# Two of 216 sender columns read from a projection kept on the chip, in place of two gathers

## The chip, the cores and the metric

One Trainium2 chip, one of its cores. The metric is the device time of one execution in microseconds (us); lower is better. The kernel is written by hand in an assembler-like language: every engine (TensorE = PE, VectorE = DVE, ScalarE = ACT, GpSimd = POOL, SyncE = SP) has its own program, and the programs meet at semaphores alone.

## The reference

A graph of 12500 nodes with 64 features each and 412500 edges (sender `src`, receiver `dst`, sorted by receiver). Two layers; the second is the one that matters here:

```
x = x + h + segment_sum(gated_mlp(edge_attr), dst)         # layer 0, h = relu(layernorm(x))
h = relu(layernorm(x))                                     # layer 1
s_proj = h @ Ws + bs ; r_proj = h @ Wr + br                # per node, 64 features (4 heads of 16)
se, re = s_proj[src], r_proj[dst]                          # per edge
logits = sum_d mish(se + re) * aw + ab                     # per edge and head
alpha = softmax of the logits over the edges of a receiver
x = x + segment_sum(alpha * se, dst)
```

`s_proj[src]` has random rows: each edge needs 64 floats (256 bytes) from some row of the table.

## The kernel before, in words

The kernel has four stages, one function each. `edge_mlp` (from the start to about 1095 us) does the gated MLP. `update_nodes` (to about 1346 us) ends layer 0, projects the nodes in 14 steps (NS) of 7 x 128 nodes, writes the sender half to the table `s_proj` in DRAM (SP, L747) and scatters the receiver half into `sums` (POOL, L762). `attention` (to about 5297 us) goes over the edges, and `finish` gathers the results.

In `attention` partition p holds 3224 consecutive edges. They are worked on in 135 chunks (CA); a chunk is 24 columns (TA), a column being one edge of each of the 128 partitions. Three buffers (B) rotate: `se` takes the 24 sender rows of each partition, `rs` the receiver rows. The loop over `s` runs 14 times (SB), and its body is written out for 3 times 3 chunks, so one iteration, called a round here, is 9 chunks or 216 columns. Three chunks go before the loop (FIRST), six after it (LAST_TWO).

Who does what for chunk c:

- POOL (`gather`, L1039 to L1048): waits until DVE has used the buffer (`se_used`) and until ACT has copied the indices, then issues one indirect DMA for each column of the chunk, each of which fetches 128 rows of 256 bytes.
- In six of the nine chunks of a round (PATTERN), the last column isn't gathered by POOL. SP and ACT load 16 row addresses at a time from `picks` into registers and issue one DMA of one row per edge into `fetched` (`fetch`, L994 and L1142: SP 5 of the 8 groups of 16, ACT the other 3), and ACT copies it into its column of `se` (L1192). `picks` holds these indices, loaded by SP in `update_nodes` (L737 to L744).
- DVE (`body`, L1249): `mish` of chunk c (L1260), then `receivers` of chunk c+1 (L1224 to L1235: it waits for `keepf_ready`, which PE's `spread_keep` gives, and scans), then `add_senders` of chunk c+1 (L1247: it waits for the gathers of that chunk, `gathered`, and for `placed`), then the softmax part of chunk c (L1266 to L1293), in which L1282 is the last reader of the sender rows and frees the buffer. The program order is fixed: nothing of a chunk can pass what stands before it.
- ACT: tanh, ln, tanh for mish (L1129, L1135, L1137), exp (L1174), copies for POOL's indices and for the stores.
- PE: `spread_keep(c+1)` (L1079) and `logits(c)` (L1088), both after `mish` of c.

In `update_nodes` a projection step is: DVE normalises 896 nodes (L822 to L838), PE transposes them (L779), ACT copies that into `hT` (L808), PE multiplies by the two weights (L784), DVE adds the bias into `sr` (L848). `sr` has four buffers, each of which has to be both stored by SP and scattered by POOL before step k+4 writes it (L843 to L845). SP's program loads `src`, then the columns of `picks`, then stores the 14 parts of the table.

Of the kernel before, what the change touches and what calls it, by code (L numbers as in the profile page):

```python
# [21 lines left out]
P = 128  # L22
N = 12500
F = 64
# [42 lines left out]
ACT_FIRST = [(0, j, g) for j in range(LEAD) for g in range(SHARE, P // GANG)]  # L67
BIG = 1e30
# [24 lines left out]
class Body:  # L93
# [22 lines left out]

    def landed(self, b):

        if isinstance(self.s, int) and self.s < 0:
            return 16 * TA  # L120
        every = sum(at[1] == b for at in PATTERN)
        here = sum(at[1] == b and at[0] <= self.u for at in PATTERN)
        if isinstance(self.s, int) and self.chunk(b) >= CA - 2:
            here += TA - TL - ((self.u, b) in PATTERN)
        return self.s * (16 * (TA * ROUND - every)) + 16 * (TA * (self.u + 2) - here)
# [5 lines left out]
def column_of(m):  # L131

    s, j = divmod(m, NPICK)
    u, b = PATTERN[j]
    return (Body(s, u).chunk(b) + 1) * TA - 1

# [536 lines left out]
def update_nodes(nc, R, A, D, gathered0):  # L673


    with ExitStack() as ctx:
# [45 lines left out]
        sr_ready = sem("sr_ready")  # L722
        tabled = [sem(f"tabled{b}") for b in range(SR)]
# [3 lines left out]
        s_tab = D["s_proj"].rearrange("(j p) f -> p j f", p=P)  # L727

        @block.sync
        def _(sp):  # L730
            sp.wait_ge(padded, 1)
            src = A["src"][0:(P - 1) * RUN].rearrange("(p k) -> p k", k=RUN)
            sp.dma_start(R["src"][0:112, :], src[0:112, :]).then_inc(src_in, 16)
            sp.dma_start(R["src"][112:P - 1, :], src[112:P - 1, :]).then_inc(src_in, 16)
            sp.dma_start(R["src"][P - 1:P, 0:LAST * T], A["src"][(P - 1) * RUN:E].rearrange("(a k) -> a k", a=1)).then_inc(src_in, 16)
            sp.wait_ge(padded, 2)
            for m in range(PICKS):  # L737
                column = A["src"][column_of(m)::RUN]
                even = column.shape[0] // GANG
                sp.dma_start(R["picks"][0:even, m, :], column[0:even * GANG].rearrange("(g q) -> g q", q=GANG), allow_slow_non_contiguous=True)\  # L740
                    .then_inc(picks_in, 16)
                if column.shape[0] < P:
                    sp.dma_start(R["picks"][even:even + 1, m, 0:GANG - 1], column[even * GANG:P - 1].rearrange("(g q) -> g q", g=1),
                                 allow_slow_non_contiguous=True).then_inc(picks_in, 16)  # L744
# [4 lines left out]
            sp.wait_ge(picks_in, 16 * (PICKS + sum(column_of(m) + (P - 1) * RUN >= E for m in range(PICKS))))  # L749
            for b in range(SR):  # L750
                sp.wait_ge(tabled[b], 16 * len(range(b, NS, SR)))
# [20 lines left out]
        @block.tensor  # L772
        def _(pe):
            nc.tensor.matmul(half_ps[:, 0:F], R["half_state"][:, :], R["ident"][0:F, 0:F], start=True, stop=True).then_inc(half_in_ps, 1)
            for k in range(NS):
                pe.wait_ge(h_ready, k + 1)
                wait(pe, hT_ready, k * len(JQ))
                for j in range(JB):
                    last = nc.tensor.transpose(hT_ps[:, j // 4, (j % 4) * P:(j % 4 + 1) * P], hh[k % 2][:, j, :], R["ident"][:, :])  # L779
                last.then_inc(hT_in_ps, 1)  # L780
                pe.wait_ge(hT_ready, (k + 1) * len(JQ))
                wait(pe, sr_ready, k)
                for j in range(JB):
                    last = nc.tensor.matmul(pr_ps[:, j // 4, (j % 4) * P:(j % 4 + 1) * P], hT[:, j, :], R["wsr"][:, :], start=True, stop=True)  # L784
                last.then_inc(pr_in_ps, 1)

        @block.scalar
        def _(act):
# [8 lines left out]
            act.wait_ge(eps_ready, 2)  # L797
            for k in range(NS // 2):
# [5 lines left out]
            for k in range(NS):  # L804
                act.wait_ge(hT_in_ps, k + 1)
                wait(act, pr_in_ps, k)
# [3 lines left out]
                if k + 1 < NS:  # L810
                    root(k + 1)

        @block.vector
        def _(dve):
# [39 lines left out]
            nc.vector.memset(R["picks"][:, :, :], 0).then_inc(padded, 1)  # L854
            pairs = [slice(2 * JB * k, 2 * JB * (k + 1)) for k in range(NS // 2)]
# [29 lines left out]
def attention(nc, R, A, D, gathered0, state_rows, states_in):  # L885

    with ExitStack() as ctx:
# [35 lines left out]
        fetched = [sb(f"fetched{j}", [P, F]) for j in range(NPICK)]  # L923
        rows = state_rows
        den = [sb(f"den{b}", [P, H, TA]) for b in range(B)]
        held_ps, ex_bank, work_ps, lg_bank = ps("held_ps", [P, 3 * 512]), ps("ex_bank", [P, 512]), ps("work_ps", [P, 3 * 512]), ps("lg_bank", [P, 512])
# [14 lines left out]
        placed = sem("placed")  # L941
        heads_in = sem("heads_in")
# [28 lines left out]
        state_out = sem("state_out")  # L971
# [66 lines left out]
        def _(pool):  # L1038
            def gather(at, b):  # L1039
# [6 lines left out]
                for k in range(EARLY if first and b == 0 else 0, TA - 1 if at.picks(b) else width(c)):  # L1046
# [18 lines left out]
        def _(pe):  # L1065
# [25 lines left out]
            def body(at, last=False):  # L1091
                for b in range(B):
# [6 lines left out]
                    logits(c)  # L1099

            pe.wait_ge(prepared, 1)
# [10 lines left out]
        def _(act):  # L1112
# [42 lines left out]
            def body(at, last=False):  # L1155
# [7 lines left out]
                for b in range(B):  # L1163
# [24 lines left out]
                    if not (last and b + 2 >= B) and ahead.picks(b2):  # L1188
# [3 lines left out]
                        nc.scalar.activation(se[b2][:, TA - 1, :], fetched[j][:, :], ACT.Copy).then_inc(placed, 1)  # L1192
                    states = rows[b][:, 0:w, 0:H * HE].rearrange("p t (h e) -> p t h e", e=HE)
# [4 lines left out]
            act.sem_inc(placed, NPICK)  # L1198
            act.wait_ge(prepared, 1)
# [12 lines left out]
        def _(dve):  # L1212
            flat = lambda x: x.rearrange("p f t -> p (f t)")
            STEP = 15

# [21 lines left out]
            def add_senders(at, b, more=True):  # L1237
# [11 lines left out]
            def body(at, last=False):  # L1249
                for b in range(B):  # L1250
# [73 lines left out]
            nc.vector.tensor_copy(R["state"][:, 0:H * HE], nlast[:, :, :].rearrange("p h e -> p (h e)")).then_inc(state_out, 1)  # L1324
            nc.vector.tensor_copy(R["state"][:, H * HE:ROW], narrow(mx[(CA - 1) % B], TL)[:, :, TL - 1]).then_inc(state_out, 1)
            dve.wait_ge(state_out, 2)


def finish(nc, R, A, D, out, states_in, ABW=F + H):

    with ExitStack() as ctx:
# [27 lines left out]
        pe_do = [sem(f"pe_do{k}") for k in range(4)]  # L1359
        pe_did = [sem(f"pe_did{k}") for k in range(4)]  # L1360
        act_do = [sem(f"act_do{k}") for k in range(2)]
        act_did = [sem(f"act_did{k}") for k in range(2)]
# [35 lines left out]
        def _(pe):  # L1398
            ident = R["ident"]
            pe.wait_ge(pe_do[0], 1)  # L1400
            nc.tensor.transpose(a_ps[0:H, 0:P], R["state"][:, F + H:ROW], ident[:, :])  # L1401
            nc.tensor.transpose(b_ps[0:H, 0:P], drop[:, :], ident[:, :]).then_inc(pe_did[0], 1)
            pe.wait_ge(pe_do[1], 1)
            nc.tensor.transpose(a_ps[:, 0:H], mx_t[:, 0:P], ident[0:H, 0:H])  # L1404
            nc.tensor.transpose(b_ps[:, 0:H], mx_t[:, 1:P + 1], ident[0:H, 0:H]).then_inc(pe_did[1], 1)
            pe.wait_ge(pe_do[2], 1)
            nc.tensor.transpose(a_ps[0:ABW, 0:P], add[:, :], ident[:, :])  # L1407
            nc.tensor.transpose(b_ps[0:ABW, 0:P], mul[:, :], ident[:, :]).then_inc(pe_did[2], 1)
            pe.wait_ge(pe_do[3], 1)
            nc.tensor.transpose(a_ps[:, 0:ABW], cin_t[:, 0:P], ident[0:ABW, 0:ABW]).then_inc(pe_did[3], 1)  # L1410

        @block.scalar
        def _(act):
            for k in range(2):
                act.wait_ge(act_do[k], 1)
                nc.scalar.activation(e[:, :, :], e[:, :, :], ACT.Exp).then_inc(act_did[k], 1)  # L1416

        @block.vector
        def _(dve):
# [10 lines left out]
            nc.vector.tensor_scalar(drop[:, :], R["whole"][:, :].to_broadcast([P, H]), -1.0, BIG, ALU.add, ALU.mult).then_inc(pe_do[0], 1)  # L1430
            dve.wait_ge(pe_did[0], 1)
            do(nc.vector.tensor_copy(drop_t[:, :], b_ps[0:H, 0:P]))  # L1432
            nc.vector.tensor_tensor_scan(mx_t[:, 1:P + 1], drop_t[:, :], a_ps[0:H, 0:P], -BIG, ALU.add, ALU.max).then_inc(pe_do[1], 1)  # L1433
            dve.wait_ge(pe_did[1], 1)
# [5 lines left out]
            nc.vector.tensor_tensor(e[:, 1, :], R["state"][:, F + H:ROW], mio[:, 1, :], ALU.subtract).then_inc(act_do[0], 1)  # L1440
            dve.wait_ge(act_did[0], 1)
# [3 lines left out]
            nc.vector.tensor_tensor(by_head(add[:, :]), by_head(R["state"][:, 0:ABW]), heads_wide(e[:, 1, :]), ALU.mult).then_inc(pe_do[2], 1)  # L1445
            dve.wait_ge(pe_did[2], 1)
            do(nc.vector.tensor_copy(mul_t[:, :], b_ps[0:ABW, 0:P]))  # L1447
            nc.vector.tensor_tensor_scan(cin_t[:, 1:P + 1], mul_t[:, :], a_ps[0:ABW, 0:P], 0.0, ALU.mult, ALU.add).then_inc(pe_do[3], 1)  # L1448
            dve.wait_ge(pe_did[3], 1)
# [5 lines left out]
            nc.vector.tensor_tensor(e[:, 1, :], mio[:, 0, :], mt[:, :], ALU.subtract).then_inc(act_do[1], 1)  # L1455
            dve.wait_ge(act_did[1], 1)
# [20 lines left out]
def gnn_program(nc, A, out):  # L1477
# [8 lines left out]
    with ExitStack() as ctx:  # L1486
# [10 lines left out]
        edge_mlp(nc, R, A, D)  # L1497
        gathered0 = ctx.enter_context(nc.semaphore("agathered0"))
# [30 lines left out]
```

## Time and profile before

| | us |
|---|---|
| three executions | 5441.60, 5443.22 (median), 5446.89 |
| the profiled execution, its own time | 5442.07 |
| its span from first to last instruction | 5439.8 |
| busy: DVE / POOL / ACT / PE | 3909.6 / 3573.8 / 2555.2 / 2022.2 |

The span is 2.3 us less than the time of the same execution, which is 1.15 us below the median. In a row of the trace a group of instructions has its busy time, the mean of one in ns, and the idle time of its engine just before it with what ended that idle time ("issue" means that nothing that the profile shows ended it: the engine was between two of its own instructions). The timeline gives start, duration, engine, line, operation, output<-input. A DMA row on SPq or ACTq is the time of issuing it, not of the transfer.

### The profile page before, as it was taken

To read this page: it belongs to the slowest core of one execution; us is meant where nothing else is said; L and a number is where in the kernel's file an instruction comes from. 1 tells how busy PE (TensorE), PEld (TensorE's weight loads), DVE (VectorE), ACT (ScalarE), POOL (GpSimd) and SP (SyncE) were. 2 spreads that over 40 slices of the span, in tenths; PEclk is the share of its full clock that TensorE was granted. 3 is DMA by queue.
4 is the path that set the end of the run, shared out by engine and by line. 5 is a ranking of instruction groups with operands and counts; after the bars stand their busy time and mean duration, and the time that the engine had idled before them with its cause. 6 is when DMAs were issued, how large, how long until landed. Compare 5 with 4: busy or idle time off the path is not lost. (4 is left out here: it accounts for less than half of the span.)

```text
span 5439.8 us, 79208 instructions
## 1 busy us (share of the span) xinstructions
PE 2022.2 (37%) x13638; PEld 1308.1 (24%) x13638; DVE 3909.6 (72%) x4216; ACT 2555.2 (47%) x3324; POOL 3573.8 (66%) x3669
## 2 busy tenths in 40 slices
PE   8999999923112222222212212212212212222220
PEld 3444444412112212212212212212212212212220
DVE  6999988853577777777776777777777777777772
ACT  7999999911243343343343443443443443343440
POOL 2444430077777777777777777777777777777756
PEclk9999999955555655656555556556556556555555
DMA  8888888721333333333333333333333333333322
GB/s 215 266 261 265 263 261 267 246 49 44 81 89 89 82 84 89 85 81 89 82 84 89 79 87 89 81 85 89 79 87 90 77 89 89 79 88 89 78 67 51
DMA packets 331213, 630.53 MB, mean 116 GB/s; under 512 B 131947, under 2 KB 135556, under 8 KB 330590
## 3 DMA queue, kind: packets, MB, share of 16 engines
q1 hardware_dynamic: 204558, 501.63, 28.6%
q0 software_dynamic: 117456, 124.66, 12.9%
q10 hardware_dynamic: 8832, 1.15, 0.2%
q14 instruction: 356, 2.92, 0.2%
q8 instruction: 11, 0.18, 0.0%
HBM read 391.98 MB, written 235.04 MB: 115 GB/s over the span
## 5 line engine op out<-in xcount | busy, mean ns | idle before, releaser
L1047 POOL DMA_INDIRECT se<-s_proj,idx x2053 | 1939.5, 945 | 626.3 <-issue 626.3
L1079 PE MATMUL held_ps<-r_keep,ident 128*128 (+2 forms) x935 | 204.9, 361 | 3056.0 <-DVE mish L1260 3026.8
L1129 ACT ACTIVATE t<-held_ps 128x1536 f32<-128x1536 f32 x135 | 194.9, 1444 | 2225.6 <-DVE held_ps L1247 2188.2
L1047 POOL DMA_INDIRECT r_se<-s_proj,idx x1012 | 955.9, 945 | 308.9 <-issue 308.0
L1079 PEld LDWEIGHTS held_ps<-r_keep,ident 128*128 128x128 bf16 x935 | 68.3, 119 | 3146.9 <-issue 2963.3
L1088 PEld LDWEIGHTS lg_bank<-mish,scaled 128*128 128x128 f32 x4320 | 740.2, 266 | 21.6 <-DVE mish L1260 9.9
L1088 PE MATMUL lg_bank<-mish,scaled 128*128 128x96 f32 (+1 forms) x4320 | 724.0, 348 | 9.7 <-DVE mish L1260 9.7
L1224 DVE SCALAR_TENSOR_TENSOR rnew<-held_ps,rs 128x1536 f32<-128x1536 f32 x135 | 374.3, 2773 | 260.0 <-PE held_ps L1079 246.8
L1247 DVE TENSOR_TENSOR held_ps<-se,held_ps 128x1536 f32<-128x1536 f32 (+1 forms) x90 | 243.7, 2708 | 412.5 <-DMA se<-s_proj,idx 395.4
L492 DVE TENSOR_TENSOR_SCAN sums<-keepb,sums,msg 128x1024 f32<-128x1024 bf16 x201 | 472.6, 2351 | 31.3 <-DVE msg L483 27.4
L427 ACT ACTIVATE hidden<-h_ps,r_b1g 128x1024 f32<-128x1024 f32 x404 | 459.5, 1138 | 7.3 <-PE h_ps L371 7.3
L1231 DVE TENSOR_TENSOR_SCAN held_ps<-held_ps,rnew 128x1536 f32<-128x1536 f32 x135 | 452.2, 3350 | 4.6
L1292 DVE TENSOR_TENSOR_SCAN work_ps<-work_ps,wse 128x1536 f32<-128x1536 f32 x135 | 452.2, 3349 | 4.6
L382 PE MATMUL v_ps<-hidden,r_w2g 64*64 64x512 f32 x1616 | 440.3, 612 | 15.3 <-issue 1.3
L383 PE MATMUL g_ps<-hidden,r_w2g 64*64 64x512 f32 x1616 | 440.2, 618 | 0.0
L371 PE MATMUL h_ps<-edges,r_w1g 64*64 64x512 f32 x3232 | 434.4, 595 | 14.5 <-DMA r_w1g<-in_L_gnn_G 7.9
L632 POOL DMA_INDIRECT nodes<-in_dst,block x102 | 167.3, 1640 | 366.7 <-DVE block L523 335.5
L434 ACT ACTIVATE value<-v_ps,b 128x512 f32<-128x512 f32 x404 | 281.4, 697 | 73.2 <-PE v_ps L382 67.6
L483 DVE SCALAR_TENSOR_TENSOR msg<-gate,value 128x1024 f32<-128x1024 f32 x202 | 246.4, 1220 | 74.5 <-ACT gate L437 73.8
L393 PE MATMUL tr_ps<-r_ident,sums 128*128 128x128 f32 x1616 | 288.1, 301 | 13.5 <-DVE sums L492 8.4
L393 PEld LDWEIGHTS tr_ps<-r_ident,sums 128*128 128x128 f32 x1616 | 211.0, 195 | 339.9 <-issue 202.1
L1260 DVE TENSOR_TENSOR mish<-held_ps,t 128x1536 f32<-128x1536 f32 x135 | 236.2, 1750 | 77.7 <-issue 42.7
(215 smaller groups left out, 4288.6 us busy)
## 6 DMA issues: line engine op xcount, KB each, us to landing
states<-arows SPq DMA_DIRECT2D x133, 864.0 KB
fetched<-s_proj SPq DMA_DIRECT2D x6960, 0.2 KB
edges<-in_edge_attr SPq DMA_DIRECT2D x202, 512.0 KB, 5.2
sums<-rows SPq DMA_DIRECT2D x402, 256.0 KB
rs<-sums SPq DMA_DIRECT2D x133, 768.0 KB, 5.2
fetched<-s_proj ACTq DMA_DIRECT2D x4176, 0.2 KB
keepb<-keep SPq DMA_DIRECT2D x404, 128.0 KB, 3.6
se<-s_proj,idx POOLq DMA_INDIRECT x2053
```

What stands on the lines that cost most here:

```text
L371: last = nc.tensor.matmul(h_ps[u][units, s, :], R["w1g1"][feats, units], edges[m][feats, half], start=True, stop=True)
L382: last_v = nc.tensor.matmul(v_ps[out, :], R["w2g2"][0:F, :], hid[0:F, s, :], start=True, stop=True)
L383: last_g = nc.tensor.matmul(g_ps[out, :], R["w2g2"][F:2 * F, :], hid[F:2 * F, s, :], start=True, stop=True)
L393: last = nc.tensor.transpose(tr_ps[:, k, j * P:(j + 1) * P], cols[:, 4 * k + j, :], R["ident"][:, :])
L427: nc.scalar.activation(hidden[u][:, :, :], h_ps[u][:, :, :], ACT.Silu, bias=R["b1g1"][:, :]).then_inc(hidden_ready, 1)
L434: nc.scalar.activation(value[m][:, half], v_ps[:, :], ACT.Silu, bias=b2[:, :]).then_inc(gated, 1)
L492: nc.vector.tensor_tensor_scan(sums[m][:, :], keepb[m][:, :], msg[m % 2][:, :], carry, ALU.mult, ALU.add).then_inc(scanned, 1)
L1047: pool.indirect_dma_start(out=se[b][:, k, :], out_offset=None, in_=D["s_proj"], in_offset=bass.IndirectOffsetOnAxis(ap=node[:, k:k + 1], a ...
L1088: last = nc.tensor.matmul(lg_ps(w), scaled[:, d, :], by_dim[:, d, :, :], start=d == 0, stop=d == HD - 1)
L1224: nc.vector.scalar_tensor_tensor(new, hold, 1.0, rs[b][:, 0:w, :].rearrange("p k f -> p f k"), ALU.subtract, ALU.mult).then_inc(rnew_ready, 1)
L1231: nc.vector.tensor_tensor_scan(held_ps[:, 0:F * w], held_ps[:, 0:F * w], flat(new), 0.0, ALU.mult, ALU.add)\
L1292: do(nc.vector.tensor_tensor_scan(work_ps[:, 0:F * w], work_ps[:, 0:F * w], flat(narrow(wse, w)), 0.0, ALU.mult, ALU.add))
```

## The change

The projected senders are also kept on the chip, transposed: `sT` is [64 features, 12544 nodes] in fp32, 49 KB in each of 64 partitions. In each step of `update_nodes` PE computes it with two more matmuls (64x64 weights, 512 and 384 columns) and ACT copies it there with the bias added.

In `attention` two more columns of the 216 of a round (COPIED: in two chunks that already have a picked column) are taken from POOL: 28 in the loop and one behind it. For such a column DVE loads 16 node numbers at a time into registers from a new tile `copied` and issues 16 copies, each of one column of `sT` (64 partitions x 1 element, at a register address) into one column of `turned` [64, 128]: 8 groups of 16 make a column of senders. PE turns it (a transpose into a PSUM bank), and ACT copies it into `se`. The groups are spread over the nine chunks of a round (1, 2, 2, 2, 1, 2, 2, 2, 2 groups), between DVE's wait for `mish` and `receivers`, some chunks ahead of their use; before the loop the first column's 8 groups go over three chunks. To free a PSUM bank the logits and the exponentials now share one (at columns 256 and 0). SP loads the 29 index columns of `copied` and the bias in `update_nodes`. Some semaphores of the tail (`finish`, and the copy of the state) are merged, with the same order of work.

```diff
+COPIED = [(0, 2), (2, 2)]
+NCOPY = len(COPIED)
+COPY_LEAD = 1
+COPIES = SB * NCOPY + COPY_LEAD
+COPY_ROWS = [(ahead, j, g) for ahead, j in [divmod(COPY_LEAD + k, NCOPY) for k in range(NCOPY)] for g in range(P // GANG)]
+COPY_FIRST = [(0, j, g) for j in range(COPY_LEAD) for g in range(P // GANG)]
...
         @block.sync
         def _(sp):
+            sp.dma_start(R["bias"][:, :], A["L1_gnn_bs"].rearrange("h d -> (h d)").rearrange("(f a) -> f a", a=1)).then_inc(bias_in, 16)
...
-            sp.wait_ge(padded, 2)
-            for m in range(PICKS):
-                column = A["src"][column_of(m)::RUN]
+            sp.wait_ge(padded, 3)
+            for tile, first in edges:
+                for m, at in enumerate(first):
+                    column = A["src"][at::RUN]
...
                 last.then_inc(pr_in_ps, 1)
+                wait(pe, t_ready, k * len(JQ))
+                for q, w in enumerate(JQ):
+                    last = nc.tensor.matmul(x_ps[0:F, q * 512:q * 512 + w * P], R["wsr"][:, 0:F],
+                                            hT[:, 4 * q:4 * q + w, :].rearrange("f j n -> f (j n)"), start=True, stop=True)
+                last.then_inc(t_in_ps, 1)
...
                 act.wait_ge(hT_in_ps, k + 1)
-                wait(act, pr_in_ps, k)
+                wait(act, t_in_ps, k)
...
                 if k + 1 < NS:
                     root(k + 1)
+                act.wait_ge(t_in_ps, k + 1)
+                for q, w in enumerate(JQ):
+                    at = (k * JB + 4 * q) * P
+                    nc.scalar.activation(R["sT"][:, at:at + w * P], x_ps[0:F, q * 512:q * 512 + w * P], ACT.Identity, bias=R["bias"][:, :])\
+                        .then_inc(t_ready, 1)
...
-        held_ps, ex_bank, work_ps, lg_bank = ps("held_ps", [P, 3 * 512]), ps("ex_bank", [P, 512]), ps("work_ps", [P, 3 * 512]), ps("lg_bank", [P, 512])
+        held_ps, heads_bank, work_ps, turn_bank = ps("held_ps", [P, 3 * 512]), ps("heads_bank", [P, 512]), ps("work_ps", [P, 3 * 512]), ps("turn_bank", [P, 512])
+        ex_bank, lg_bank = heads_bank[:, 0:H * TA], heads_bank[:, 256:256 + H * TA]
...
-                for k in range(EARLY if first and b == 0 else 0, TA - 1 if at.picks(b) else width(c)):
+                for k in range(EARLY if first and b == 0 else 0, width(c) - at.others(b)):
                     pool.indirect_dma_start(out=se[b][:, k, :], out_offset=None, in_=D["s_proj"],
...
                     logits(c)
-
+                    ahead, b2 = at.after(b + 2)
+                    if not (last and b + 2 >= B) and ahead.copies(b2):
+                        m, j = ahead.copy(b2), COPIED.index((ahead.u, b2))
+                        pe.wait_ge(copied, m + 1)
+                        pe.sem_inc(pe_turn, 1)
+                        pe.wait_ge(copy_placed, m + 1)
+                        pe.sem_inc(pe_turn, 1)
+                        nc.tensor.transpose(turn_bank[:, 0:F], turned[j][:, :], R["ident"][0:F, 0:F]).then_inc(copy_turned, 1)
...
                         nc.scalar.activation(se[b2][:, TA - 1, :], fetched[j][:, :], ACT.Copy).then_inc(placed, 1)
+                    if not (last and b + 2 >= B) and ahead.copies(b2):
+                        j = COPIED.index((ahead.u, b2))
+                        wait(act, se_used, c)
+                        act.wait_ge(copy_turned, ahead.copy(b2) + NCOPY + 1)
+                        nc.scalar.activation(se[b2][:, copied_column(j), :], turn_bank[:, 0:F], ACT.Copy).then_inc(copy_placed, 1)
...
+            def copy(s, pieces):
+
+                for ahead, j, g in pieces:
+                    m = (s + ahead) * NCOPY + j
+                    if g == 0:
+                        dve.wait_ge(copy_turned, m + 1)
+                        dve.sem_inc(copy_turn, 1)
+                    nodes = [dve.alloc_register(f"copy{'' if isinstance(s, int) else 's'}{ahead}_{j}_{g}_{q}") for q in range(GANG)]
+                    dve.reg_load(nodes, R["copied"][g:g + 1, bass.ds(m, 1), :].rearrange("a i q -> a (i q)"))
+                    for q in range(GANG):
+                        at = dve.snap(nodes[q], donate=True, min_val=0, max_val=NN - 1)
+                        last = nc.vector.tensor_copy(turned[j][:, g * GANG + q:g * GANG + q + 1], R["sT"][:, bass.ds(at, 1)])
+                    if g == P // GANG - 1:
+                        last.then_inc(copied, 1)
...
+                if at.copies(b):
+                    dve.wait_ge(copy_placed, at.copy(b) + 2)
                 if more:
                     dve.wait_ge(rlast_ready, c + 1)
...
                     if not ending:
                         dve.wait_ge(mish_ready, c + 1)
+                        copy(0 if at is FIRST else at.s, copy_lots[b])
                         receivers(at, b + 1, more=not (last and b + 2 == B))
                         add_senders(at, b + 1, more=not (last and b + 2 == B))
```

## Rows read from the trace of the kernel before

**Rows 1.** The page's parts 1 and 2: busy time, and tenths busy in 40 slices

```profile
PE 2022.2 (37%) x13638; PEld 1308.1 (24%) x13638; DVE 3909.6 (72%) x4216; ACT 2555.2 (47%) x3324; POOL 3573.8 (66%) x3669
...
POOL 2444430077777777777777777777777777777756
```

**Rows 2.** Waits in 1500 to 5300 us: who waited for whom, total, times, longest

```profile
DVE held_ps L1247 <- DMA se<-s_proj,idx: 392.9, 85, 7.9
...
DVE rnew L1224 <- PE held_ps L1079: 239.7, 130, 1.9
DVE held_ps L1247 <- DMA r_se<-s_proj,idx: 179.4, 43, 6.0
```

**Rows 3.** POOL's gathers in 1500 to 5300 us, grouped by line

```profile
L1047 POOL DMA_INDIRECT se<-s_proj,idx x2025 | 1913.1, 945 | 617.7 <-issue 617.7
```

**Rows 4.** Timeline of attention, parts of two chunks

```profile
3004.04 2.78 DVE L1224 SCALAR_TENSOR_TENSOR rnew<-held_ps,rs 128x1536 f32<-128x1536 f32 x1 [1.85 <-PE held_ps L1079]
...
3011.17 0.94 POOL L1047 DMA_INDIRECT r_se<-s_proj,idx  x1 [0.30 <-issue]
...
3015.78 2.73 DVE L1247 TENSOR_TENSOR held_ps<-se,held_ps 128x1536 f32<-128x1536 f32 x1 [4.63 <-DMA se<-s_proj,idx]
...
3018.41 0.30 DVE L1266 TENSOR_SCALAR lgb<-lg_bank,r_ab 128x96 f32<-128x96 f32 x1
...
3018.84 0.23 DVE L1267 SCALAR_TENSOR_TENSOR lgb<-mx,kn,lgb 128x4 f32<-128x4 f32 x1
...
3046.86 0.26 DVE L1281 COPY dse<-ex_bank 128x96 f32<-128x96 f32 x1 [0.38 <-ACT ex_bank L1174]
...
3047.15 2.75 DVE L1282 TENSOR_TENSOR wse<-se,ex_bank 128x1536 f32<-128x1536 f32 x1
```

**Rows 5.** SP's issues on both sides of one load of 16 registers

```profile
3017.58 0.55 SPq L1005 DMA_DIRECT2D fetched<-s_proj  x2
...
3019.50 0.27 SPq L1005 DMA_DIRECT2D fetched<-s_proj  x1
```

**Rows 6.** Lines L1315 and L1290: ns min/median/max of one, first and last start

```profile
L1315 DVE TENSOR_SCALAR scaled<-r_ident,r_aw x16: 268/274/476, 1350.6 to 1353.6; 128x128 f32<-128x128 f32 x16
...
L1290 DVE COPY nlast<-den x135: 170/171/409, 1418.7 to 5293.6; 128x4 f32<-128x4 f32 x135
```

**Rows 7.** Small operations of DVE by line and form, whole span

```profile
L1442 DVE TENSOR_SCALAR e<-e,r_whole 128x4 f32<-128x4 f32 x1 | 0.2, 229 | 0.3 <-ACT e L1416 0.3
...
L1444 DVE COPY mul<-e 128x68 f32<-128x68 f32 x1 | 0.2, 196 | 0.0
...
L1439 DVE TENSOR_SCALAR e<-e 128x4 f32<-128x4 f32 x1 | 0.2, 170 | 0.0
...
L1325 DVE COPY r_state<-mx 128x4 f32<-128x4 f32 x1 | 0.2, 163 | 0.0
```

**Rows 8.** POOL's timeline while L1315 runs on DVE

```profile
1351.30 1.01 POOL L767 DMA_INDIRECT r_se<-s_proj,r_src  x1 [0.31 <-issue]
1352.61 0.94 POOL L767 DMA_INDIRECT r_se<-s_proj,r_src  x1 [0.30 <-issue]
```

**Rows 9.** Timeline of one projection step in update_nodes

```profile
1171.29 3.35 PE L784 MATMUL pr_ps<-r_wsr,hT 64*128 64x128 f32 x14 [1.05 <-ACT hT L808]
...
1178.68 1.70 PE L779 MATMUL hT_ps<-r_ident,hh 128*64 128x128 f32 x7 [4.04 <-DVE hh L838]
...
1180.42 0.96 ACT L808 ACTIVATE hT<-hT_ps 64x512 f32<-64x512 f32 x2 [3.35 <-PE hT_ps L779]
```

**Rows 10.** Groups of 1080 to 1480 us, then SP's issues in the timeline

```profile
L762 POOL DMA_INDIRECT sums<-sr,r_start x98 | 95.6, 976 | 29.9 <-issue 29.9
...
L848 DVE TENSOR_TENSOR sr<-pr_ps,r_bsr 128x512 f32<-128x512 f32 (+1 forms) x28 | 17.5, 624 | 83.9 <-PE pr_ps L784 55.2 <-DMA sums<-sr,r_start 28.2
...
1099.65 60.50 SPq L740 DMA_DIRECT2D r_picks<-in_src  x81
...
1166.04 157.18 SPq L747 DMA_DIRECT2D s_proj<-sr  x14
```

More of the change, by code:

```diff
@@ L115, in pick, with copies, copy, others @@
         return self.s * NPICK + PATTERN.index((self.u, b))
+    def copies(self, b):
+        if isinstance(self.s, int) and (self.s < 0 or self.chunk(b) >= CA - 2):
+            return False
+        return (self.u, b) in COPIED
+    def copy(self, b):
+        return self.s * NCOPY + COPIED.index((self.u, b))
+    def others(self, b):
+        return self.picks(b) + self.copies(b)
     def landed(self, b):
@@ L120, in landed @@
             return 16 * TA
-        every = sum(at[1] == b for at in PATTERN)
-        here = sum(at[1] == b and at[0] <= self.u for at in PATTERN)
+        every = sum(at[1] == b for at in PATTERN + COPIED)
+        here = sum(at[1] == b and at[0] <= self.u for at in PATTERN + COPIED)
         if isinstance(self.s, int) and self.chunk(b) >= CA - 2:
-            here += TA - TL - ((self.u, b) in PATTERN)
+            here += TA - TL - ((self.u, b) in PATTERN) - ((self.u, b) in COPIED)
         return self.s * (16 * (TA * ROUND - every)) + 16 * (TA * (self.u + 2) - here)
@@ L135, in column_of, with copied_column, copied_edges @@
     return (Body(s, u).chunk(b) + 1) * TA - 1
+def copied_column(j):
+    return TA - 1 - (COPIED[j] in PATTERN)
+def copied_edges(m):
+    s, j = divmod(m, NCOPY)
+    u, b = COPIED[j]
+    return Body(s, u).chunk(b) * TA + copied_column(j)
 def wait(eng, sem, value):
@@ L748, in _ @@
             sp.wait_ge(src_in, 48)
-            sp.wait_ge(picks_in, 16 * (PICKS + sum(column_of(m) + (P - 1) * RUN >= E for m in range(PICKS))))
+            sp.wait_ge(picks_in, 16 * sum(1 + (at + (P - 1) * RUN >= E) for _, first in edges for at in first))
             for b in range(SR):
@@ L1249, in body @@
             def body(at, last=False):
+                if at is FIRST:
+                    copy_lots = [part(COPY_FIRST, b, B) for b in range(B)]
+                elif isinstance(at.s, int) and at.s == SB:
+                    copy_lots = [[] for b in range(B)]
+                else:
+                    copy_lots = [part(COPY_ROWS, at.u * B + b, ROUND * B) for b in range(B)]
                 for b in range(B):
@@ L1358, in finish @@
         chain = sem("chain")
[L1359 to L1362, printed above, removed]
+        pe_do = sem("pe_do")
+        pe_did = sem("pe_did")
+        act_do = sem("act_do")
+        act_did = sem("act_did")
         got_in = sem("got_in")
@@ L1414, in _ @@
             for k in range(2):
-                act.wait_ge(act_do[k], 1)
-                nc.scalar.activation(e[:, :, :], e[:, :, :], ACT.Exp).then_inc(act_did[k], 1)
+                act.wait_ge(act_do, k + 1)
+                nc.scalar.activation(e[:, :, :], e[:, :, :], ACT.Exp).then_inc(act_did, 1)
         @block.vector
@@ L1497, in gnn_program @@
         edge_mlp(nc, R, A, D)
+        for name, shape, dt in [("sT", [F, NN], f32), ("copied", [P // GANG, COPIES, GANG], i32), ("bias", [F, 1], f32)]:
+            R[name] = ctx.enter_context(nc.sbuf_tensor(f"r_{name}", shape, dt))
         gathered0 = ctx.enter_context(nc.semaphore("agathered0"))
```

72 lines of the change are left out of this document (42 added, 30 removed).

## The prediction

> **What bounds the kernel.** I read the page's busy line and slices first [rows 1]. DVE is the busiest engine with 3909.6 us, which invites the wrong answer: POOL has only 3573.8, but its digit is a flat 7 from the ninth slice to the end. The reader should ask what POOL's other three tenths are. The group of its gathers answers [rows 3]: 1913.1 us busy and 617.7 us idle for 2025 gathers, all of the idle time put down to "issue". So POOL waits for nobody; one gather costs (1913.1 + 617.7) / 2025 = 1.250 us, start to start. A round of the loop has 216 columns less 6 picked ones, 210 gathers or 262.5 us.
>
> DVE, in contrast, waits for POOL's gathers [rows 2]: 392.9 + 179.4 = 572.3 us over the 130 chunks of that stretch, 4.40 us a chunk, and for PE's spreading of the keep flags 239.7 us, 1.84 us a chunk. That is 56.2 us of wait in a round, and DVE's own path is 262.5 - 56.2 = 206.3 us. The timeline shows how the two are tied [rows 4]: the senders of a chunk are in at 3015.78, 4.6 us after POOL left that chunk at 3011.17; DVE frees that buffer at 3049.9 (L1282), and POOL, with two more chunks of 23 or 24 gathers to do, wants it only about 58 us after 3011.17. DVE can be some 19 us late in one chunk without stopping POOL; only its mean over a round matters.
>
> **Step 1, removed: gathers.** 28 columns in the loop and one behind it leave POOL: 29 x 1.250 = 36.2 us. POOL's round becomes 208 x 1.250 = 260.0 us. Everything before, behind and between stays on POOL's line.
>
> **Step 2, added to DVE.** A round gets 16 groups, each a load of 16 registers and 16 copies of 64x1 at register addresses. The load: SP's issues end at 3018.13 and start again at 3019.50 around such a load [rows 5], 1.37 us, of which about 0.1 would be there anyway; I take 1.3 us, as SP's is the nearest. The copy: the trace has no row of it. From below: the operation with a computed address, L1267, starts 0.13 us after the end of the one before it, where L1282 starts 0.03 us behind L1281 [rows 4], so an address costs the sequencer 0.10 us. The engine's own pace comes from L1315, 16 operations with no wait between them, whose starts are 3.0 / 15 = 0.20 us apart [rows 6]. They carry 128 columns, 0.066 us by 196 - 163 ns for 64 more columns, and a scalar operand, 0.059 us by 229 - 170 ns [rows 7]; without both, 0.075 us. If the two run side by side a copy costs 0.10 us and a little; one after the other, 0.175 us. L1315's durations of 274 ns overlap at 200 ns, so they run side by side: I take 0.12 us, bounds 0.075 (the address work vanishing, too) and 0.175.
>
> A group is 1.3 + 16 x 0.12 = 3.2 us, 16 groups 51.5 us, and the two waits with their signals 0.5: 52 us. The groups stand right behind mish, where PE's spreading runs beside them, so the 1.84 us wait is covered (each chunk has at least one group), and the rest comes out of the wait for gathers. DVE's round: 206.3 + 52 = 258.3 us, against POOL's 260.0. POOL stays the bound by 1.7 us, a very thin cover. What is queued behind the copies is receivers, add_senders and so ACT's tanh, logits and POOL's buffer; all of it is late only where DVE's mean passes POOL's.
>
> In its own sentences: the Trainium skill ("VectorE: DVE Perf Modes", the TRN2 errata section) states 58 cycles plus the elements at 0.96 GHz for an SBUF to SBUF operation, an estimate of 61 ns for this copy. By it the sum would be about 15 us less of DVE work in a round; the trace shows no copy under 160 ns in duration, and no pitch of one.
>
> **Step 3, contention between the copies and POOL.** L1290, a small fp32 copy from SBUF to SBUF, takes 171 ns as a rule and up to 409 [rows 6]; something held it for 0.24 us. While L1315 ran densely for 3 us, one of POOL's gathers took 1.01 us in place of 0.94 and the next 0.94 [rows 8]. So POOL loses 0 to 0.07 us for each gather that dense small operations cover. The copies last 29 x 128 x 0.12 = 445 us, 356 gathers; at 0.03 us each 11 us, bounds 0 and 25.
>
> **Step 4, PE and ACT in attention.** One transpose and one 64-column copy on ACT, 29 times; ACT does the like for picked columns and waits on DVE for most of a chunk. Both stand behind logits and in front of a wait for DVE: nothing. If DVE became the bound they would still be off its path.
>
> **Step 5, update_nodes.** Two matmuls over 896 columns, the size of L784's seven, 3.35 us; they end 3.35 us after 1174.64, before PE's next transposes at 1178.68, and two copies on ACT of 0.96 us fit into its idle 3.35 us [rows 9]. Should the step grow by 1 us all the same, POOL's scatters cover it: all 98 have no idle time but issue, and DVE waits 28.2 us for the fourth of them [rows 10]. SP's index loads: 81 take 60.5 us, 0.75 each; the 29 new columns, 2 short tails and the bias are 32 x 0.75 = 24 us, so SP is at its first table store at about 1190 in place of 1166.04, where the buffer is needed again only by the fifth step, held by the scatters to 1229. No cost; without that cover 24 us. One memset on DVE: under 1 us. The renamed semaphores and the shared bank: nothing, since logits, L1278 and exp already follow one another.
>
> **Sum.** 5442.07 - 36.2 + 11 + 1 = 5418 us for the execution profiled, which is 1.15 below the median: 5419. The change can be told from none above 0.2%, 11 us.
>
> **Rivals.**
> (a) VectorE becomes the bound, and the kernel is slower. Place: the copies between mish and receivers. It decides from the point where 16 groups cost more than 53.7 us, and the kernel is slower than before above 56.2, which is 0.136 us for a copy. For it: margins of a few per cent, a register load that SP shows and not DVE, and a round of some 560 more instructions to fetch. Against it: the address work of 0.10. At 0.155 us a copy a group is 3.78, the round 267.3, 4.8 x 14 = 67 us more than before: 5510. At 0.175 it is 5580; at 0.20, 5670. If it comes to pass, the waits for gathers vanish and POOL waits for `se_used`. Chance 0.27.
> (b) The copies lock POOL out. Each gather that they cover waits for a whole copy, 0.17 us [rows 6]: 356 x 0.17 = 60 us, 24 us more than the gain: 5467; at half of that 5437. For it: L1290's 409; against it: the gathers beside L1315 [rows 8]. Chance 0.10.
> The Trainium skill ("SBUF — State Buffer", who interferes with whom) says that an fp32 copy from SBUF to SBUF uses the port that GpSimd writes its descriptors through, and that the one that comes second is blocked for the whole instruction. By that rule the trace agrees in kind (409 ns), and the one gather of 1.01 us speaks for a small size.
> (c) A tie: DVE at 260 to 262.5 us a round, within 0.2% of before: 5432 to 5450. Chance 0.13.
> That the change doesn't do what it says is out for the gathers, whose count is in the code; that POOL's gathers don't set the pace is contradicted by [rows 2, 3].
>
> **Numbers.** The forecast, POOL still the bound and 12 to 36 us gained, has 0.50. Faster by over 0.2%: 0.50 and a little of (b), 0.52; the same: (c) and part of (b), 0.17; slower: (a) and the rest of (b), 0.31. The range goes from 5404 (the full 36.2 and no contention) to 5520, which leaves out (a) above 0.16 us a copy. The likeliest case by itself is 5405 to 5432.
>
> **What would show it.** Right: 29 gathers fewer, their pitch 1.25 to 1.26 us with POOL's idle time all "issue"; DVE's wait for gathers down to almost nothing but there; a loop round of 260 to 261 us. Wrong: POOL idle behind L1282 (rival a, with the group's cost readable from the gap between mish and L1224), gathers of over 1.0 us under the copies (rival b), a later end of update_nodes (step 5).

## The result, and the profile of the changed kernel

| | before | after |
|---|---|---|
| median of four executions, us | 5444.34 | 5404.71 (5402.85 to 5407.04) |
| the profiled execution: its own time / its span, us | 5442.07 / 5439.8 | 5402.85 / 5401.0 |
| loop round: mean of twelve, DVE / POOL, us | 262.45 / 262.46 (210 gathers of 1.2498) | 259.94 / 259.91 |

The ratio is 0.9928, interval 0.991 to 0.9945: faster by 0.7%. The forecast was 5419 in a range of 5404 to 5520, its likeliest case by itself 5405 to 5432. The 5443.22 that stands with the kernel before is the median of its first three executions. A round is read here from the start of its first mish product to that of the next round's, and for POOL between its gathers in the same places.

The page of the kernel after, parts 1 and 2, answers to [rows 1]:

```profile
PE 2074.6 (38%) x13723; PEld 1324.3 (25%) x13723; DVE 4344.4 (80%) x7930; ACT 2573.8 (48%) x3381; POOL 3544.2 (66%) x3640
...
DVE  6999998863688888888888888888888888888872
...
POOL 2444430067777777777777777777777777777756
```

DVE has 434.8 us more of work and the kernel is 39 us shorter: what bounds a kernel isn't the busiest row. POOL's row is as flat as before.

Waits of DVE from 1500 to 5300 us after, answering to [rows 2] (who waited for what: total us, times, longest):

```profile
DVE turned L1296 <- issue: 312.7, 279, 1.6
...
DVE mish L1352 <- issue: 43.2, 13, 3.6
...
DVE held_ps L1333 <- DMA se<-s_proj,idx: 11.0, 4, 4.2
DVE rnew L1308 <- PE held_ps L1133: 7.7, 5, 1.7
```

The wait for gathers was 572.3 us and is 13.3 (11.0, and 2.3 in another row); the one for PE's spreading was 239.7 and is 7.7. In their place DVE copies. Most of the 312.7 us in front of the copies is its sequencer loading registers: the trace has 232 such loads, and one takes 1.10 us. Some 18 us are pauses of 0.32 to 0.35 us between two copies of a group. DVE has hardly a wait left in a round. What stays is a pause of 3.3 us in front of mish once in each round of the loop, as long as a whole group; it was there before (42.7 us, 13 times).

POOL's gathers in the same stretch after, as [rows 3]:

```profile
L1101 POOL DMA_INDIRECT se<-s_proj,idx x1995 | 1884.6, 945 | 608.7 <-issue 603.8 <-DVE wse L1375 4.9
L1101 POOL DMA_INDIRECT r_se<-s_proj,idx x989 | 933.6, 944 | 301.7 <-issue 294.1 <-DVE wse L1375 7.6
```

All gathers together: (1884.6 + 608.7 + 933.6 + 301.7) / 2984 = 1.2495 us from start to start, against 1.2498 before. The 12.5 us put down to DVE are 41 gaps of 0.3 us, as long as any other gap between two gathers, so nothing was waited for. In attention there are 3100 gathers in place of 3129. The first starts at 1354.61 us (before 1356.35), the last ends at 5227.85 (before 5266.6), and 173.2 us lie behind it in both.

DVE's timeline in attention after, two groups in one chunk (start, duration, engine, line, operation; in brackets the idle time before it):

```profile
3015.15 1.76 DVE L1352 TENSOR_TENSOR mish<-held_ps,t 128x1536 f32<-128x1536 f32 x1 [0.24 <-DVE nlast L1386]
3018.27 1.86 DVE L1296 COPY turned<-r_sT 64x1 f32 x16 [1.36 <-issue]
3021.34 1.86 DVE L1296 COPY turned<-r_sT 64x1 f32 x16 [1.20 <-issue]
3023.31 2.74 DVE L1308 SCALAR_TENSOR_TENSOR rnew<-held_ps,rs 128x1536 f32<-128x1536 f32 x1
3026.19 0.38 DVE L1312 SCALAR_TENSOR_TENSOR rnew<-rs,km,rlast 128x64 f32<-128x64 f32 x1
```

A group costs 3021.34 - 3018.27 = 3.07 us: 1.2 for the load and 1.86 for sixteen copies, 0.116 each. Over a round, DVE's work without any group is 207.1 us; that is the round of 260.2 us of the kernel with the copies left out (below), less what its waits for gathers and for PE are longer than a usual pause. So sixteen groups cost 259.9 - 207.1 = 52.8 us, 3.3 each. The 0.2 us more than in the timeline stands in what a chunk pays once, some 0.26 us (1.36 in place of 1.20 us in front of the first group, 0.1 in front of rnew), and in about four pauses of 0.3 us a round between two copies.

Durations in ns (least/median/most), first and last start, of the copies and of the small operation that was L1290 in [rows 6]:

```profile
L1296 DVE COPY turned<-r_sT x3712: 144/146/148, 1388.8 to 5102.2; 64x1 f32 x196
...
L1383 DVE COPY nlast<-den x135: 171/172/385, 1416.7 to 5255.5; 128x4 f32<-128x4 f32 x135
```

Of 3712 copies, none took over 148 ns.

Update_nodes, groups of 1080 to 1480 us after, then SP's issues, as [rows 10]:

```profile
L799 POOL DMA_INDIRECT sums<-sr,r_start x98 | 95.6, 976 | 29.9 <-issue 29.9
...
L896 DVE TENSOR_TENSOR sr<-pr_ps,r_bsr 128x512 f32<-128x512 f32 (+1 forms) x28 | 17.5, 625 | 82.6 <-PE pr_ps L821 55.2 <-DMA sums<-sr,r_start 26.9
...
1164.82 20.02 SPq L777 DMA_DIRECT2D r_copied<-in_src  x28
...
1187.39 8.82 SPq L784 DMA_DIRECT2D s_proj<-sr  x4
```

The scatters wait for nothing, DVE's waits are those of before, and SP is at its first table store 21 us later than before, at nobody's cost.

### The profile page after: what moved, and what is told of

Its sections match the earlier page's. It is cut to its first block and busy times, and to the rows that moved or that the text cites. A ratio compares the mean times of both kernels' runs of the same rounds, so it can differ in the third digit from the quotient of the medians.

```text
span 5401.0 us, 87509 instructions
## 1 busy us (share of the span) xinstructions
PE 2074.6 (38%) x13723; PEld 1324.3 (25%) x13723; DVE 4344.4 (80%) x7930; ACT 2573.8 (48%) x3381; POOL 3544.2 (66%) x3640
## 5 line engine op out<-in xcount | busy, mean ns | idle before, releaser
L1101 POOL DMA_INDIRECT se<-s_proj,idx x2024 | 1912.1, 945 | 617.5 <-issue 612.4
L1142 PEld LDWEIGHTS heads_bank<-mish,scaled 128*128 128x128 f32 x4320 | 742.9, 267 | 22.4 <-DVE mish L1352 10.7
L1142 PE MATMUL heads_bank<-mish,scaled 128*128 128x96 f32 (+1 forms) x4320 | 726.5, 349 | 10.5 <-DVE mish L1352 10.5
L1296 DVE COPY turned<-r_sT 64x1 f32 x3712 | 434.2, 146 | 323.8 <-issue 323.8
L1315 DVE TENSOR_TENSOR_SCAN held_ps<-held_ps,rnew 128x1536 f32<-128x1536 f32 x135 | 452.2, 3350 | 4.6
```

What stands on the lines that cost most here:

```text
L1101: pool.indirect_dma_start(out=se[b][:, k, :], out_offset=None, in_=D["s_proj"], in_offset=bass.IndirectOffsetOnAxis(ap=node[:, k:k + 1], a ...
L1142: last = nc.tensor.matmul(lg_ps(w), scaled[:, d, :], by_dim[:, d, :, :], start=d == 0, stop=d == HD - 1)
L1296: last = nc.vector.tensor_copy(turned[j][:, g * GANG + q:g * GANG + q + 1], R["sT"][:, bass.ds(at, 1)])
L1315: nc.vector.tensor_tensor_scan(held_ps[:, 0:F * w], held_ps[:, 0:F * w], flat(new), 0.0, ALU.mult, ALU.add)\
```

## Experiments

Two batches of four and one single run. Each was compared with the kernel before on the same chip; its median was 5442.22, 5441.94 and 5446.31 us. "The kernel after" stands for 5404.71 and 0.9928; it ran beside a kernel before of 5444.34, so a difference in us between a run here and it is good to 2 to 4 us.

**Copies left out.** What do the copies cost?

```diff
-                    nodes = [dve.alloc_register(...) for q in range(GANG)]
-                    dve.reg_load(nodes, ...)
-                    for q in range(GANG):
-                        at = dve.snap(nodes[q], ...)
-                        last = nc.vector.tensor_copy(turned[j][...], R["sT"][:, bass.ds(at, 1)])
                     if g == P // GANG - 1:
-                        last.then_inc(copied, 1)
+                        dve.sem_inc(copied, 1)
```

> The changed kernel without DVE's register loads and copies (their signals stay; the two copied columns of a round hold zeros, so that part of the result is not computed). Theory A, POOL's gathers set the pace and the copies only fill DVE's wait: 5404 us as with the copies (within 4), POOL's gathers 1.250 us apart, and DVE waits again for gathers and PE, some 53 us in a round. Rival B, DVE has become a second bound: clearly under 5400, since 53 us of work in a round are gone.

Measured: 5405.81 us (5403.72 to 5407.54), ratio 0.9931 [0.9914, 0.9947]. DVE's waits, 1500 to 5300 us:

```profile
DVE held_ps L1328 <- DMA se<-s_proj,idx: 402.3, 86, 7.4
DVE rnew L1303 <- PE held_ps L1133: 240.3, 130, 1.9
DVE held_ps L1328 <- DMA r_se<-s_proj,idx: 129.7, 41, 5.7
```

Without a single copy the kernel takes the same time, and the waits that the copies had filled are back: 532.0 us for gathers, 240.3 for PE, 54 us a round where some 53 were expected. The copies lie wholly inside DVE's waits and slow nothing else; POOL's pitch here is 1.2507 us, not shorter than beside the copies.

**Gathers kept.** Everything is added, but POOL gathers the two columns too; the turned column goes to a tile that nobody reads.

```diff
-        return self.picks(b) + self.copies(b)
+        return int(self.picks(b))
...
-                        nc.scalar.activation(se[b2][:, copied_column(j), :], turn_bank[:, 0:F], ACT.Copy).then_inc(copy_placed, 1)
+                        nc.scalar.activation(aside[:, :], turn_bank[:, 0:F], ACT.Copy).then_inc(copy_placed, 1)
```

> Everything that the change adds (the projection kept on the chip, index loads, register loads, copies, turns), but POOL gathers the two columns all the same and ACT puts the turned ones aside. Theory A: 5443 us, the time of the kernel before, since DVE's round of 259.9 us fits under 210 gathers (262.5 us); DVE waits 2 to 3 us in a round for gathers. Rival B or a cost in update_nodes: over 5450. Rival C, the gain of 39 us comes from something other than the 29 gathers (a bank, a semaphore): well under 5440.

Measured: 5440.45 us (5438.38 to 5446.01, ten executions), ratio 0.9996 [0.9987, 1.0006]. All that the change adds costs nothing that 0.1% can show; all of the gain is the gathers. DVE's waits, 1500 to 5260 us:

```profile
DVE held_ps L1334 <- DMA se<-s_proj,idx: 50.4, 16, 4.3
```

A second row has 4.8 us. Not all of this is the loop's steady state: in the twelve rounds over which a round is read here (1749.4 to 4899.9 us, 262.55 us each) the first row is 34.2 us and the second is empty, 2.85 us a round, within the 2 to 3 expected. DVE's own path, with the same program as after, is therefore 262.55 - 2.85 = 259.7 us. (The execution profiled was the slowest of the ten, 5446.01 us, with POOL's pitch at 1.2510.) This is the best measure of the cover: 259.9 - 259.7 = 0.2 us a round, next to nothing.

**One column.**

```diff
-COPIED = [(0, 2), (2, 2)]
+COPIED = [(0, 2)]
```

> Only column (0, 2) of a round is copied, 15 in all. Theory A: 14 gathers more than with two columns, 17.5 us: 5422. DVE waits for gathers again, about 23 us in a round. Rival B: nearer to 5404 or below, since DVE loses 26 us of work in a round.

Measured: 5422.61 us (5421.49 to 5423.21), ratio 0.9963 [0.9949, 0.9978]: 19.6 us less than before and 17.9 more than after. Fourteen columns and one are 15 x 1.250 = 18.8 us. Each column is worth its gathers, the second as much as the first as far as can be told. DVE's waits for gathers, 1500 to 5300 us, are 374.7 us, 26 a round where 23 were expected.

**Three columns.** (1, 2) is added, the groups in the same place: the forecast's rival (a), forced.

```diff
-COPIED = [(0, 2), (2, 2)]
+COPIED = [(0, 2), (1, 2), (2, 2)]
```

> A third column (1, 2) copied in each round: 24 groups. Theory A with DVE at its limit: DVE's round is 207.1 + 24 x 3.3 = 286 us against POOL's 207 x 1.25 = 258.7, so (286 - 259.9) x 14 = 370 us more than with two: about 5770, and POOL waits for the release of its buffers. If DVE had room left: 5387.

Measured: 5741.58 us (5736.08 to 5742.64), ratio 1.0547 [1.0529, 1.0565]. POOL's waits, 1500 to 5260 us, and two lines of its timeline:

```profile
POOL se L1101 <- DVE wse L1375: 238.6, 76, 3.9
POOL r_se L1101 <- DVE wse L1375: 117.4, 38, 5.3
```

```profile
3023.89 0.94 POOL L1101 DMA_INDIRECT se<-s_proj,idx  x1 [0.30 <-issue]
3026.96 1.00 POOL L1101 DMA_INDIRECT r_se<-s_proj,idx  x1 [2.12 <-DVE wse L1375]
```

Now POOL waits at the head of chunks for DVE to free a buffer (2.12 us here), 356 us in all, and DVE's row of waits for gathers is gone from its list. The round is 284.7 us = 207.1 + 24 x 3.23: the price of a group holds, and from 53 us of groups on each one is paid in full.

**Copies of two elements.** Does a bigger copy meet POOL where the small one doesn't?

```diff
-                        last = nc.vector.tensor_copy(turned[j][:, g * GANG + q:g * GANG + q + 1], R["sT"][:, bass.ds(at, 1)])
+                        last = nc.vector.tensor_copy(turned[j][:, g * GANG + q, :], R["sT"][:, bass.ds(at, 2)])
```

> Each of the 3712 copies moves two elements a partition (node and its neighbour) in place of one; the second is not used. Theory D: the copies of one element escaped the contention with POOL only by their size (none of 3632 took over 160 ns, while the 4-element copy took up to 409 ns); with two elements some are held by 0.04 to 0.24 us, and POOL's gathers under them grow by 0.03 to 0.1 us: DVE's round passes 260, 5410 to 5450. Rival E: small copies don't meet POOL at all, or the engine catches up: 5404, all durations alike.

Measured: 5405.49 us (5401.92 to 5410.79), ratio 0.993 [0.9913, 0.9946]. Durations of the copies, ns:

```profile
L1297 DVE COPY turned<-r_sT x3712: 150/161/422, 1391.7 to 5110.1; 64x2 f32 x196
```

Copies up to 422 ns appear, where those of one element had 148 at most. Of the 3712 copies 911 took over 15 ns more than the median. They are those that start 0.5 to 0.75 us into a gather (694 of 742) or close to the start of the next. In the kernel after, 760 copies of one element start 0.5 to 0.75 us into a gather, and none is longer for it. The time doesn't show the holds: POOL's pitch stays 1.2504 us, and the starts of the copies lie as far apart as in the kernel after (256 of them take 39.96 us of a round in both), since the sequencer sets that pace and a held copy is caught up with. So the half of theory D on the copies came true, the half on the gathers and the time didn't. DVE's round is 260.3 us against POOL's 260.1, though: DVE starts its sender addition 7.6 us behind POOL's last gather of the chunk early in the loop and 10.1 late in it. What is longer is not the copies but one pause a round in front of the sender addition, 0.46 us where the kernel after has 0.1; with no cover, that is enough.

**Loads ahead of the wait for mish.** Both loads of a chunk are issued while mish runs.

```diff
+                        nodes = load(0 if at is FIRST else at.s, copy_lots[b])
                         dve.wait_ge(mish_ready, c + 1)
-                        copy(0 if at is FIRST else at.s, copy_lots[b])
+                        copy(0 if at is FIRST else at.s, copy_lots[b], nodes)
```

> Both register loads of a chunk are issued ahead of DVE's wait for mish, so that up to 1.76 us of them runs beside that operation. Theory A: the time stays, 5404, because POOL sets it, and DVE gets 9 x 1.7 = 15 us of waits for gathers back in a round (the sum of its waits in 1500 to 5250 us rises from 13 us to some 200). Rival B: 5380 or less.

Measured: 5403.43 us (5402.25 to 5404.39), ratio 0.9929 [0.9912, 0.9945]: no gain, as POOL still sets the round. DVE's waits, 1500 to 5300 us:

```profile
DVE held_ps L1340 <- DMA se<-s_proj,idx: 218.0, 64, 4.7
DVE turned L1303 <- DVE mish L1359: 75.5, 97, 0.9
...
DVE turned L1303 <- issue: 33.2, 70, 1.1
```

It makes room, though: the wait for gathers is back with 222.9 us, about 15 a round as expected, 1.0 for each group. The load of registers is what a group pays without need.

**Groups apart, two columns.** The first group of a chunk stays behind mish, with its load ahead; the second goes behind the start of rnew.

```diff
                                                ALU.subtract, ALU.mult).then_inc(rnew_ready, 1)
+                copy(turn_s, lot[0:1])
                 dve.wait_ge(rnew_ready, c + 1)
```

> Two columns, the first group of a chunk behind mish with its load ahead of the wait, the second behind the start of rnew, so that its load runs beside that operation. Theory A: 5404 again, and DVE's waits for gathers rise to about 16 x 1.15 = 18 us in a round.

Measured: 5406.41 us (5405.37 to 5409.28), ratio 0.9933 [0.9917, 0.995]. DVE's waits, 1500 to 5300 us:

```profile
DVE held_ps L1344 <- DMA se<-s_proj,idx: 322.6, 69, 7.4
DVE held_ps L1344 <- DMA r_se<-s_proj,idx: 84.2, 34, 4.8
```

406.8 us, 28 a round: more room than with loads ahead alone, again without a gain in time.

**Groups apart, three columns.** The room is used: as the last, with COPIED of three, and a third place behind the start of the scan into `held_ps`.

```diff
                 nc.vector.tensor_tensor_scan(held_ps[...], held_ps[...], flat(new), 0.0, ALU.mult, ALU.add).then_inc(held, 1)
+                copy(turn_s, lot[1:2])
                 dve.wait_ge(held, c + 1)
```

> Three columns, at most one group behind mish, one beside rnew and one beside the scan, all loads hidden. Theory A: DVE's round is 207.1 + 24 x 2.1 = 257.5 us, just under POOL's 207 x 1.25 = 258.7: 14 more gathers gone, 17.5 us, 5387. If the loads can't hide there, 5404 to 5740.

Measured: 5389.59 us (5387.53 to 5390.29), ratio 0.9903 [0.9887, 0.992]. The interval overlaps that of the kernel after, but no execution of the one reaches into those of the other. DVE's timeline:

```profile
3002.44 1.76 DVE L1363 TENSOR_TENSOR mish<-held_ps,t 128x1536 f32<-128x1536 f32 x1 [0.23 <-DVE nlast L1399]
3004.33 1.86 DVE L1305 COPY turned<-r_sT 64x1 f32 x16
3006.27 2.78 DVE L1317 SCALAR_TENSOR_TENSOR rnew<-held_ps,rs 128x1536 f32<-128x1536 f32 x1
3008.96 1.05 DVE L1305 COPY turned<-r_sT 64x1 f32 x16
3009.93 0.36 DVE L1322 SCALAR_TENSOR_TENSOR rnew<-rs,km,rlast 128x64 f32<-128x64 f32 x1
```

The group behind mish still takes 1.86 us: its load is hidden, but a wait stands in front of its address work. The one behind rnew takes 1.05: the sequencer, with no wait between, worked the addresses out while rnew ran, and the engine runs sixteen copies at a pitch of (1.05 - 0.14) / 15 = 0.06 us. A round is 258.8 us, 22 of it waits for gathers: (258.8 - 22.0 - 207.1) / 24 = 1.24 us a group, in place of 3.3 (and of the 2.1 expected). This is a mean of two kinds. A group behind mish takes 2.07 us (from mish's end at 3004.20 to 3006.27), but 1.85 of that was DVE's wait for PE before [rows 4]. One behind rnew adds 0.8: L1322 starts 3009.93 - 3006.27 = 3.66 us after rnew, and in the kernel after, with no group there, 3026.19 - 3023.31 = 2.88.

**Four columns.** COPIED is (0, 2), (1, 1), (2, 0), (2, 2), with a fourth place behind the sender addition.

```diff
                         add_senders(at, b + 1, more=not (last and b + 2 == B))
+                        copy(turn_s, lot[3:4])
```

> Four of 216 sender columns are copied by VectorE, in 32 groups of 16 a round of nine chunks, with up to four groups in a chunk at four places: behind the mish product, behind the start of rnew, behind the held scan and behind the sender addition. Theory A (GpSimd's gathers set the round as long as VectorE's work with hidden loads stays under them): 206 gathers x 1.250 = 257.5 us a round, VectorE 207.1 + 32 x 1.24 = 247, so 14 rounds save about 14 x 1.25 = 17.5 us against three columns: about 5372 us, VectorE still waits some 10 us a round for gathers. Rival B (the group hides only where a long operation stands ahead of it; the fourth place has the short sender addition ahead, and costs 3.3 us a group there): VectorE 207.1 + 24 x 1.24 + 8 x 3.3 = 263 us a round, over GpSimd's 257.5: about 5450 us, with no wait for gathers left. Rival C (some of each: the fourth place costs about 2 us a group): VectorE 253, same 5372 us, but only some 4 us of waits a round.

Measured: 5372.19 us (5367.47 to 5379.92), ratio 0.9869 [0.9852, 0.9887], the fastest version found. Waits of DVE, 1500 to 5300 us, its timeline, and POOL's gathers from 1500 to 5200:

```profile
DVE held_ps L1344 <- DMA se<-s_proj,idx: 177.2, 66, 5.5
```

```profile
3010.07 2.73 DVE L1344 TENSOR_TENSOR held_ps<-r_se,held_ps 128x1536 f32<-128x1536 f32 x1
3012.70 1.05 DVE L1305 COPY turned<-r_sT 64x1 f32 x16
3013.67 0.30 DVE L1373 TENSOR_SCALAR lgb<-heads_bank,r_ab 128x96 f32<-128x96 f32 x1
```

```profile
L1101 POOL DMA_INDIRECT se<-s_proj,idx x1980 | 1870.7, 945 | 604.1 <-issue 602.0 <-DVE wse L1389 2.1
```

The fourth group is nearly as cheap as the one behind rnew, so rival B falls: L1373 starts 3.60 us after the sender addition where [rows 4] have 2.63 (3018.41 - 3015.78), 1.0 us for a group. So 2.7 us of sender addition cover a load and sixteen addresses. The round is 257.5 us = 206 x 1.250, 12.6 of it waits of DVE for gathers; a group costs (257.5 - 12.6 - 207.1) / 32 = 1.18 us. Theory A's 5372 is what came, and 12 us a round of waits speak against rival C's 4. Five columns weren't tried; by these numbers DVE (207.1 + 40 x 1.18 = 254) and POOL (256.3) would be nearly even.

## Why the prediction was right

**What bounds the kernel: right.** Gathers kept costs nothing and gains nothing, copies left out gains as much as the change: POOL's pitch times its gathers is the round, before and after.

**Step 1, 36.2 us: right.** From the first gather to the last, attention is 37.0 us shorter: (5266.6 - 1356.35) - (5227.85 - 1354.61). That is 29 gathers, and 0.8 us of a slightly shorter pitch.

**Step 2, DVE's round: every term near, but the cover of 1.7 us was gone.** The load was taken at 1.3 us, from SP's; on DVE it is 1.10 by itself and 1.1 to 1.4 with the pauses around it. The copy was taken at 0.12 and is 0.116: the reading that addresses and copies run side by side, and that the address work, not the engine, sets the pace, is shown by the pitch of 0.06 where that work is hidden. Sixteen groups were 52 us and are 52.8; DVE without them 206.3, and 207.1. Two small errors of 0.8 us each use up 1.6 of the 1.7 us: DVE's round is 259.7 (gathers kept) to 259.9 us, and POOL's is 259.9. POOL does still set the time, as copies left out shows, but with nothing to spare: 0.1 us more for a group would have made a round 1.6 us longer and the kernel 22. That the forecast held here is in part luck. The Trainium skill ("VectorE: DVE Perf Modes", the TRN2 errata section) gives by its formula an estimate of 61 ns for such a copy: that is the pitch behind a long operation, and neither the duration (146 ns) nor the pitch of this change (116 ns). A sum made with it would have come out right in time, as POOL sets that, but with 15 us a round of room that wasn't there. Three columns in the same place would by it have been 206.3 + 24 x (1.3 + 16 x 0.061) + 0.7 = 261.7 us a round, an estimate of some 25 us more than two columns. They cost 337 us.

**Step 3, contention, 11 us: the term that was mis-sized. It is 0.** It rested on two rows, the 409 ns of L1290 and one gather of 1.01 us in [rows 8]. The first was read rightly as an operation held by POOL, but it has 4 elements; copies of one element aren't held (0 of 3712), and those of two are. The other direction, gathers held by copies, doesn't show at all: 1.2495 us with them, 1.2498 before and 1.2507 with the copies left out. Within the kernel after, the 238 gathers beside which eight or more copies start take 0.943 us, and those beside none 0.945. The gather of 1.01 us is there again in the kernel after, beside the same sixteen operations of 128 elements; it was no evidence for copies of one.

**Steps 4 and 5, nothing: right.** The index loads, the two matmuls and ACT's copies stand in the cover that was named; not one of them has a cost in the gathers-kept run. Only the size of one term differed: the stages before attention end 1.7 us sooner where 1 us more was allowed. That is within the spread from run to run: in the traces here, POOL's first fetch of sender rows starts anywhere from 1341.1 to 1345.8 us (before 1344.9, after 1343.1).

**The sum.** With contention at its measured value the working gives 5442.07 - 36.2 + 0 + 1 = 5406.9; less 2.7 (those stages) and 0.8 (the pitch) it is 5403.4, and 5402.85 was measured. The range's lower end, said to be the full 36.2 us and no contention, should have been 5443.2 - 36.2 = 5407.0 and not 5404: that the median of 5404.71 lies inside owes something to this slip.

**The rivals.** (a) had its place, its price and its turning point right, and was one column away: three columns in the same place made POOL wait for L1375, as described. Its sign "the waits for gathers vanish" came to pass in the changed kernel too, without its cost; what decided was the second sign, POOL idle. (b) falls. The Trainium skill ("SBUF — State Buffer", who interferes with whom) says that a copy can run in a mode that takes the port pair which DVE shares with GpSimd, and that the second of the two to come is then blocked for the whole instruction. By that rule the trace agrees for two and four elements in one direction, with up to about 0.26 us for a copy, less than a gather's 0.94, and not for one element or for the gathers. (c) came close in DVE's round, 259.9 us where its tie begins at 260. Its times of 5432 to 5450 don't follow from that, as at 260 us all 29 gathers are still gained.

## What to carry to other kernels

Where two engines each have a nearly fixed round, add up both rounds, and price a move by the difference that it leaves: here two columns came off free, because their groups fitted into waits of some 53 us, with 0 to 0.2 us left over, and the next group would have cost its full 3.2 us. A margin of 1.7 us in 260 is less than the errors of such a sum. Before such a cover is given up as full, look at where the small operations stand: directly behind a long operation (2.7 us or more here), with no wait between them, register loads and address work vanish, and the same group costs 0.8 to 1.0 us in place of 3.3. The profile shows what can be hidden so as idle time put down to "issue" in front of small operations.

## What the runs showed that was not expected

**Copies of one element were never held, those of two were.** In these runs one element in each of 64 partitions takes 144 to 148 ns, never held; two elements: median 161, up to 422; four elements in 128 partitions: median 172, up to 385. Why one element passes was not tried, and neither was an odd number above one.

**The price of a register address.** A copy's duration is 146 ns, its pitch 116 with the address work in front of it and 60 with that work hidden; durations and even single-instruction pitches don't add up to what a sequence costs.

**Two engines in step without a wait.** After the change DVE's round is 259.94 us and POOL's 259.91, and neither waits for the other. DVE's lag stays the same as well: at one and the same chunk of a round, its sender addition starts 7.3 to 7.4 us behind POOL's last gather from the fourth round to the last. DVE's own path with gathers kept is 259.7 us, so no hidden cost is needed to explain 259.9. L1383 is held by up to 213 ns in 35 of 135 chunks (L1290 in 18 before), 4.3 us in all; that is 0.3 us a round, and as much with gathers kept, so it doesn't tell the two apart. Whether something couples the two engines, or two equal rounds met by chance, stays open.
